# Attention and feed-forward layer: projections, bilinear keys and turns put into the 64-row and 64-column matmul shapes

## The chip, the cores and the metric

The kernel runs on 1 core of one Trainium2 chip. The metric is the device time of one execution in microseconds (us).

## The reference

Input x is 8 batches of 1024 rows of 256 numbers, all fp32. What is computed:

```python
x = x + attn(layernorm(x))          # 16 heads of 64, no mask
x = x + ffn(layernorm(x))

# attn: xn = layernorm(x) * gamma
q, k, v = xn @ Wq, split(xn @ Wkv)              # 256 -> 1024 each
q, k = rotary(q) / 8, rotary(k)
kt = einsum('bhnd,hde->bhne', k, W_bilinear)    # 64 x 64 per head
out = softmax(q @ kt.T) @ v                     # 1024 x 1024 per head
return out @ Wo
# ffn: layernorm, ternary w1 (256 -> 1024), gelu, layernorm, ternary w2
```

## The kernel before, in words

There are three stages. `prologue` normalises and turns the first batch and splits the projection weights into a high and a low part (each product of such operands is three fp32r matmuls: high by high, low by high, high by low). `feed_forward` runs over row tiles at the end. Between them stands `attention`, which the change is about.

`attention` runs over T = 64 pairs of heads (8 batches x 8 pairs). The loop body is `span(k, t, b)`, written out for each engine, and a span does three things at once, for different pairs: `attn` is the softmax and the value products of pair t, `prep` finds the row maxima of pair t + 1, and `proj` makes q, k, v of pair t + 2. In the first two spans (k = -2 and -1) there is no `attn`, in the last two no `proj`, so 62 spans do all three. A span has four quads (q = 0 to 3). On TensorE (the PE) each quad is, in this order:

- the score stage: 36 matmuls of 64 rows by 128 columns, issued in pairs for the two heads (L715 to L731 scores, L773 max scores). The eight max-score matmuls go to the banks X[0], X[1], M, X[0], X[1], M, X[0], X[1]; VectorE (DVE) reduces each (L654) and that frees the bank, which `x_red` counts.
- the projection stage, in 128 rows by 128 columns: K in q = 0 and Q in q = 1 (L834, 6 matmuls of 512 columns into M for the first half of the tokens, c = 0, then 6 into X[0] for the second, c = 1), V in q = 2 (L853, 12 matmuls of 256 columns into M, then 12 into X[0]) and two turns of the next x tile (L860), the bilinear keys in q = 3 (L877, one fp32 matmul into M, one into X[0]). q = 1 and q = 3 end with a turn of the maxima (L778).
- the value stage, in 128 rows by 64 columns, fp32: in q = 0 and q = 2 first the sums of the probabilities into M (L786), then 8 value products in pairs for the two heads (L910). An fp32 matmul shows as two records.

What releases what around the projections: DVE's `rotate` (L642 product with the cosines, L644 with the sines) reads c = 0 from M, then c = 1 from X[0]. The sums of q = 0 write M, and wait for `rotate` to have read it; the sums of q = 2 wait for ScalarE's copy of the c = 0 half of V (L514):

```python
if q == 0 and k >= 1:
    if proj:
        wait(pe, sin_made[K], 2 * pp + 1)
...
if q == 2:
    if proj:
        wait(pe, v_copied, 2 * pp + 1)
```

DVE then takes the reciprocal of the sums (L567). SyncE (SP) issues every DMA of the stage in one written order. GpSimd (POOL) adds the probabilities (L422), adds the rotated halves (L428) and multiplies the outputs by the reciprocals (L433).

## Time and profile before

| | |
|---|---|
| time, median of 3 runs | 3566.96 us (3565.94 to 3568.25) |
| span of the profiled execution | 3566.5 us |
| PE busy | 3472.3 us, 97% of the span |
| DVE busy | 2841.1 us, 80% |
| POOL busy | 2784.1 us, 78% |
| ACT busy | 2283.5 us, 64% |
| DMA | 321.71 MB, mean 90 GB/s |

The span is the time from the first to the last instruction of one profiled execution; no time of that execution beyond its span is given, and the median of the timed runs is 0.5 us above the span. Matmuls are pipelined: a record of PE lasts longer than the step from one matmul to the next, so the pace is read from the starts, and idle time of the PE is counted from the modelled end of the record before.

### The profile page before, as it was taken

How to read it: one execution, taken by the hardware profiler on the slowest of the kernel's cores; microseconds unless marked ns; L12 is line 12 of the kernel's file. 1: busy time of each engine (PE TensorE's matmuls, PEld its weight loads, DVE VectorE, ACT ScalarE, POOL GpSimd, SP SyncE). 2: the span in 40 equal slices, each digit the busy share in tenths (PEclk: the TensorE clock that was granted, in tenths of full speed). 3: DMA queues.
4: the chain of work that ended last, by engine and by line, in shares of the span. 5: the costliest groups of instructions: out<-in, count | busy, mean ns of one | idle time of the engine just before them, and what ended most of it. 6: DMA issues, size and time to landing. Idle time of an engine off the chain costs nothing. (4 is left out here: it accounts for less than half of the span.)

```text
span 3566.5 us, 70837 instructions
## 1 busy us (share of the span) xinstructions
PE 3472.3 (97%) x21150; PEld 2250.9 (63%) x21150; DVE 2841.1 (80%) x4376; ACT 2283.5 (64%) x4340; POOL 2784.1 (78%) x1407
## 2 busy tenths in 40 slices
PE   6999999999999999999999999999999996999999
PEld 4656655665555556555565555566666663888888
DVE  6778777778777777777777777887777777899998
ACT  2666666666666666666666666666666664555555
POOL 2999999999998899999999998999999995222222
PEclk8999999999999999999999999999999998999999
DMA  5222222222222222322222222222222112333332
GB/s 197 84 82 104 88 82 79 78 103 87 87 85 102 85 87 83 106 87 85 82 105 87 87 84 101 87 87 87 104 77 75 59 62 88 92 97 96 97 95 69
DMA packets 219697, 321.71 MB, mean 90 GB/s; under 512 B 20832, under 2 KB 144224, under 8 KB 214880
## 3 DMA queue, kind: packets, MB, share of 16 engines
q1 hardware_dynamic: 210144, 309.28, 25.5%
q10 hardware_dynamic: 9216, 8.39, 0.7%
q8 instruction: 156, 2.56, 0.3%
q14 instruction: 181, 1.48, 0.1%
HBM read 186.52 MB, written 61.60 MB: 70 GB/s over the span
## 5 line engine op out<-in xcount | busy, mean ns | idle before, releaser
L422 POOL TENSOR_TENSOR prob_sum<-prob_sum,prob 128x1024 f32<-128x1024 f32 x762 | 1883.6, 2472 | 248.0 <-ACT prob L506 204.7
L506 ACT ACTIVATE prob<-scores 128x512 f32<-128x512 f32 x2048 | 1072.0, 600 | 572.6 <-PE scores L724 557.8
L654 DVE TENSOR_REDUCE row_max<-max_scores 128x1 f32<-128x512 f32 x1536 | 988.3, 685 | 285.7 <-PE max_scores L773 267.7
L910 PE MATMUL attn_out<-prob,v 128*64 128x512 f32 x4096 | 930.8, 596 | 0.0
L715 PE MATMUL scores<-q_hi,k_hi 64*128 64x512 f32 x2048 | 782.6, 415 | 7.0 <-ACT scores L477 3.9
L724 PE MATMUL scores<-q_lo,k_hi 64*128 64x512 f32 x2048 | 752.8, 393 | 1.3 <-issue 1.3
L720 PE MATMUL scores<-q_hi,k_lo 64*128 64x512 f32 x2048 | 753.5, 394 | 0.0
L910 PEld LDWEIGHTS attn_out<-prob,v 128*64 128x64 f32 x4096 | 285.0, 137 | 557.5 <-issue 556.6
L773 PE MATMUL max_scores<-k_hi,q_hi 64*128 64x512 f32 x1536 | 578.1, 429 | 7.2 <-DVE rows L644 3.0
L477 ACT ACTIVATE scores<-neg_max_seeds 128x512 f32<-128x512 f32 x1024 | 553.3, 603 | 7.6 <-DMA neg_max_seeds<-neg_max_halves 7.6
L715 PEld LDWEIGHTS scores<-q_hi,k_hi 64*128 64x128 f32 x2048 | 376.4, 185 | 275.3 <-issue 159.0
L567 DVE RECIPROCAL sum_inverted<-shared 128x512 f32<-128x512 f32 x128 | 428.8, 3350 | 32.4 <-PE shared L786 32.3
L731 PE MATMUL scores<-neg_max,ones_rows 64*128 64x512 f32 x1024 | 397.1, 389 | 0.0
L724 PEld LDWEIGHTS scores<-q_lo,k_hi 64*128 64x128 f32 x2048 | 374.4, 185 | 24.8 <-issue 1.8
L720 PEld LDWEIGHTS scores<-q_hi,k_lo 64*128 64x128 f32 x2048 | 358.2, 185 | 16.0
L1044 POOL TENSOR_TENSOR up_scale<-veps_b,halfpow 128x1 f32<-128x1 f32 x64 | 35.1, 549 | 426.5 <-DVE up_biased L1173 402.7
L654 DVE TENSOR_REDUCE row_max<-shared 128x1 f32<-128x512 f32 x512 | 348.6, 681 | 0.1
L428 POOL TENSOR_TENSOR rows<-rows 128x1024 f32<-128x1024 f32 x128 | 305.3, 2385 | 28.3 <-DMA rows<-rows 28.3
L422 POOL TENSOR_TENSOR prob_sum<-prob 128x1024 f32<-128x1024 f32 x127 | 304.5, 2398 | 24.0 <-ACT prob L506 24.0
L773 PEld LDWEIGHTS max_scores<-k_hi,q_hi 64*128 64x128 f32 x1536 | 264.8, 185 | 42.3 <-DVE row_max L654 8.9
L834 PE MATMUL shared<-xt_batch,w_group 128*128 128x512 f32 x768 | 218.0, 420 | 11.8 <-issue 8.1
L773 PE MATMUL shared<-k_hi,q_hi 64*128 64x512 f32 x512 | 201.3, 393 | 0.3
(137 smaller groups left out, 5005.7 us busy)
## 6 DMA issues: line engine op xcount, KB each, us to landing
rows<-rows SPq DMA_DIRECT2D x512, 128.0 KB, 2.0
neg_max_seeds<-neg_max_halves SPq DMA_DIRECT2D x128, 512.0 KB, 3.8
w_group<-w_parts SPq DMA_DIRECT2D x30, 1536.0 KB, 6.9
attn_normalised<-z_stage SPq DMA_DIRECT2D x128, 256.0 KB, 2.0
v<-attn_normalised SPq DMA_DIRECT2D x64, 512.0 KB, 4.1
x_turned_parts<-x_tile_parts SPq DMA_DIRECT2D x49, 256.0 KB, 3.0
xt_batch<-x_turned_parts SPq DMA_DIRECT2D x7, 1792.0 KB, 11.2
x_in<-in_x SPq DMA_DIRECT2D x64, 128.0 KB, 3.8
```

The lines of the kernel that those rows point to most:

```text
L422: nc.gpsimd.tensor_tensor(psums[half][:, :, :], a, prob[:, n % RING, :, :], ALU.add).then_inc(added, 1)
L428: nc.gpsimd.tensor_tensor(rot[x][:, :], rot[x][:, :], swapped[x][:, :], ALU.add).then_inc(rot_made[x], 1)
L477: nc.scalar.activation(S[e][i][:, :], seeds[:, h, e, :], ACT.Copy).then_inc(seeded[e], 1)
L506: nc.scalar.activation(prob[:, n % RING, e, :], S[e][n % 2][:, :], ACT.Exp).then_inc(exped[e], 1)
L567: nc.vector.reciprocal(inv[:, :], M[:, :]).then_inc(inv_made, 1)
L654: nc.vector.reduce_max(mx[1 - u][:, e, n // 2, n % 2:n % 2 + 1], bank_of(e, jj)[:, :], axis=AX.X)\
L715: nc.tensor.matmul(out, KH[u][rows(e), keys], QH[u][rows(e), q], start=n % 4 >= SEEDED, stop=False, skip_group_check=True)
L720: nc.tensor.matmul(out, KL[u][rows(e), keys], QH[u][rows(e), q], start=False, stop=False, skip_group_check=True)
L724: last = nc.tensor.matmul(out, KH[u][rows(e), keys], QL[u][rows(e), q], start=False, stop=n % 4 < SEEDED, skip_group_check=True)
L731: nc.tensor.matmul(out, onesr[rows(e), :], NM[rows(e), q], start=False, stop=True, skip_group_check=True).then_inc(s_made[e], 1)
L773: nc.tensor.matmul(bank_of(e, jj)[:, :], QH[v][rows(e), tile * P:(tile + 1) * P], KH[v][rows(e), cols(part)], start=True, stop=True).then_ ...
L910: nc.tensor.matmul(O[rows(e), :], V[k // 2 % 2][:, j, col:col + DH], prob[:, n % RING, e, :], start=j == 0, stop=j == 7).then_inc(pv_made[ ...
```

## The change

Every matmul of the attention stage and of the prologue gets one of the two shapes of the score stage (64 rows by 128 columns) and the value stage (128 rows by 64 columns).

- The projections are cut into 64-row halves. Rows 0 to 63 of the array take the tokens of c = 0 and write M, rows 64 to 127 take those of c = 1 and write X[0]. The contraction over 256 is four steps of 64 (NK = 4) instead of two of 128, so K and Q are 12 pairs of matmuls each, and V is 24 pairs; the two halves are interleaved, c = 1 first. The wait ahead of them is one for both banks.
- Input (`XT`) and weights (`W`) are laid out for this: the input's upper partitions hold the second half of the tokens; the weights stand twice, in both halves of the partitions, so there is one buffer of 3 MB in place of two of 1.5 MB. It is refilled in three parts (`next_w`), each as soon as the projection that reads it is done.
- Keys, the turns of the maxima and of x are fp32 matmuls of 64 columns with the identity or the bilinear blocks, in place of full-width ones and of transposes.
- In the prologue only the first group of weights is split at once; three groups, in place of two, are split at the start of `attention` and written to memory in six DMAs each.

```diff
         @blk.tensor
         def _(pe):
-            pe.wait_ge(small_in, 32)
-            for u in two:
-                pe.wait_ge(x_normed, ST * (u + 1))
-                for k in range(KT):
-                    for i in range(ST):
-                        last = nc.tensor.transpose(bank[u][k][:, i * P:(i + 1) * P], xn[u][:, i, k * P:(k + 1) * P], ident[:, :])
-                last.then_inc(x_turned, 1)
+            pe.wait_ge(small_in, 48)
+            pe.wait_ge(x_normed, 2 * ST)
+            for k in quads:
+                for i in range(ST):
+                    for u in two:
+                        last = nc.tensor.matmul(bank[k][u * DH:(u + 1) * DH, i * P:(i + 1) * P],
+                                                xn[u][:, i, k * DH:(k + 1) * DH], ident[:, :], start=True, stop=True)
+                        if i == ST - 1:
+                            last.then_inc(x_turned, 1)
...
-            def load_w(group, u):
-                sp.dma_start(W[u][:, :, :, :].bitcast(F), w_scr[group]).then_inc(w_in[u], 16)
+            def load_w(group, x):
+                for c in two:
+                    sp.dma_start(W[rows(c), x].bitcast(F), w_scr[group, x]).then_inc(w_in[x], 16)
...
-                sp.dma_start(xt_scr[(b + (k + 2) // PAIRS - k // PAIRS + 1) & (B - 1), :, :, :, cols],
-                             xparts[k % 2][:, :, :, :].bitcast(F)).then_inc(x_stored[k % 2], 16)
+                for j in two:
+                    sp.dma_start(xt_scr[(b + (k + 2) // PAIRS - k // PAIRS + 1) & (B - 1), r // 4, :, :, j::2, cols],
+                                 xparts[k % 2][rows(j), :, :, :].bitcast(F)).then_inc(x_stored[k % 2], 16)
...
-                sp.dma_start(XT[:, :, :, 0:N - P].bitcast(F), xt_scr[b, :, :, :, 0:N - P]).then_inc(xt_in, 16)
+                for c, done in zip(two, (HALF, HALF - P)):
+                    sp.dma_start(XT[rows(c), :, :, 0:done].bitcast(F), xt_scr[b, c, :, :, :, 0:done]).then_inc(xt_in, 16)
...
+            def next_w(k, t, x):
+
+                p = (k + 2) % PAIRS
+                if p % 2 == 0 or k >= T - 3:
+                    return
+                for c in two:
+                    wait(sp, proj_made[x][c] if x < 2 else v_made[c], t + 3)
+                    at_rest()
+                group = (p // 2 + 1) % GROUPS
+                if k < PAIRS - 2:
+                    sp.wait_ge(w_out[group], 16 if group == 0 else 16 * 6)
+                load_w(group, 1 - x if x < 2 else 2)
+
+            def store_late(g):
+
+                wait_late(g)
+                for x in range(3):
+                    for j in two:
+                        sp.dma_start(w_scr[1 + g, x, :, :, j::2, :], stage[g % 2][rows(j), :, :, x * 2 * P:(x + 1) * 2 * P].bitcast(F))\
+                            .then_inc(w_out[1 + g], 16)
...
-                    if p % 2 and k < T - 6:
-                        wait(sp, v_made, 2 * (t + 2) + 2)
-                        at_rest()
-                        if k == -1:
-                            sp.wait_ge(w_out, 16 * GROUPS)
-                        load_w((p // 2 + 2) % (PAIRS // 2), (p // 2) % 2)
+                    next_w(k, t, 2)
...
-                    for g in two:
-                        sp.wait_ge(late_lo, g + 1)
-                        sp.dma_start(w_scr[2 + g], stage[g].bitcast(F)).then_inc(w_out, 16)
+                    store_late(0)
+                    sp.dma_start(late[0], late_src).then_inc(late_in[0], 16)
+                    store_late(1)
                     sp.wait_ge(zeroed, 5)
+                if k == -1:
+                    store_late(2)
             pairs(sp, span)
...
+                if k == -1:
+                    act.wait_ge(w_out[1], 16 * 6)
+                    late_high(2)
                 if k == 0:
-                    act.wait_ge(w_out, 16 * GROUPS)
+                    for g in (2, 3):
+                        act.wait_ge(w_out[g], 16 * 6)
...
-                            wait(act, v_made, 2 * (t + 2) + c + 1)
+                            wait(act, v_made[c], t + 3)
...
-                            tile = 4 * u + 2 * c
+                            tile = 4 * c + 2 * u
...
-                    wait(dve, proj_made[x], 2 * (t + 2) + c + 1)
+                    wait(dve, proj_made[x][c], t + 3)
...
-                nc.tensor.transpose(X[1][:, 0:P], negm[:, :], ident[:, :]).then_inc(nm_turned, 1)
+                nc.tensor.matmul(X[1][rows(0), 0:P], negm[:, rows(0)], ident[:, :], start=True, stop=True).then_inc(nm_turned, 1)
...
-                order = [(xp, wp, c) for xp, wp in ((0, 0), (1, 0), (0, 1)) for c in range(KT)]
+                order = [(xp, wp, c) for xp, wp in ((0, 0), (1, 0), (0, 1)) for c in range(NK)]
...
-                        for c in two:
-                            out = (M if c == 0 else X[0])[:, :]
-                            if q == K and c == 0:
-                                batch = b + (k + 2) // PAIRS - k // PAIRS
-                                if p % 2 == 0 and k > 0:
-                                    pe.wait_ge(w_in[p // 2 % 2], 16 * (2 * batch + p // 4))
-                                if p == 0 and k > 0:
-                                    pe.wait_ge(xt_in, 16 * batch)
-                                    wait(pe, x_stored[1], 64 * batch)
-                                wait(pe, lo_made[K], 2 * (t + 1) + 1)
-                                wait(pe, x_red[1], 16 * (t + 1) + 2)
-                            elif q == Q and c == 0:
-                                if not prep:
-                                    wait(pe, sin_made[K], 2 * pp + 1)
-                                wait(pe, x_red[1], 16 * (t + 1) + 6)
-                            else:
-                                wait(pe, x_red[1], 16 * (t + 1) + 4 * q + 3)
-                                if q == Q and not prep:
-                                    wait(pe, sin_made[K], 2 * pp + 2)
-                            base = 2 * P * (1 - q) + P * (p % 2)
-                            for m, (xp, wp, kt) in enumerate(order):
-                                last = nc.tensor.matmul(out, w[:, wp, kt, base:base + P], XT[:, xp, kt, cols(c)],
-                                                        start=m == 0, stop=m == len(order) - 1)
-                            last.then_inc(proj_made[q], 1)
+                        if q == K:
+                            batch = b + (k + 2) // PAIRS - k // PAIRS
...
+                            wait(pe, lo_made[K], 2 * (t + 1) + 1)
+                        if p % 2 == 0 and k > -2:
+                            pe.wait_ge(w_in[1 - q], 32 * (GROUPS * (b + (k + 2) // PAIRS - k // PAIRS) + p // 2))
+                        if q == Q and not prep:
+                            wait(pe, sin_made[K], 2 * pp + 2)
+                        wait(pe, x_red[1], 16 * (t + 1) + 4 * q + 3)
+                        for m, (xp, wp, kt) in enumerate(order):
+                            for c in (1, 0):
+                                last = nc.tensor.matmul((X[0] if c else M)[:, :], W[rows(c), 1 - q, wp, kt, P * (p % 2):P * (p % 2) + P],
+                                                        XT[rows(c), xp, kt, :], start=m == 0, stop=m == last_step)
+                                if m == last_step:
+                                    last.then_inc(proj_made[q][c], 1)
...
-                        for c in two:
-                            bank = M if c == 0 else X[0]
-                            if c == 0:
-                                if not prep:
-                                    wait(pe, sin_made[Q], 2 * pp + 1)
-                                wait(pe, x_red[1], 16 * (t + 1) + 10)
-                            else:
-                                wait(pe, x_red[1], 16 * (t + 1) + 4 * q + 3)
-                                if not prep:
-                                    wait(pe, sin_made[Q], 2 * pp + 2)
-                            for a in two:
-                                j = 4 * u + 2 * c + a
-                                for m, (xp, wp, kt) in enumerate(order):
-                                    last = nc.tensor.matmul(bank[:, a * 2 * P:(a + 1) * 2 * P], XT[:, xp, kt, j * P:(j + 1) * P],
-                                                            w[:, wp, kt, 4 * P:6 * P], start=m == 0, stop=m == len(order) - 1)
-                            last.then_inc(v_made, 1)
+                        if p % 2 == 0 and k > -2:
+                            pe.wait_ge(w_in[2], 32 * (GROUPS * (b + (k + 2) // PAIRS - k // PAIRS) + p // 2))
+                        if not prep:
+                            wait(pe, sin_made[Q], 2 * pp + 2)
+                        wait(pe, x_red[1], 16 * (t + 1) + 11)
+                        for a in two:
+                            j = (2 * u + a) * P
+                            for m, (xp, wp, kt) in enumerate(order):
+                                for c in (1, 0):
+                                    last = nc.tensor.matmul((X[0] if c else M)[:, a * 2 * P:(a + 1) * 2 * P], XT[rows(c), xp, kt, j:j + P],
+                                                            W[rows(c), 2, wp, kt, :], start=m == 0, stop=m == last_step)
+                                    if a and m == last_step:
+                                        last.then_inc(v_made[c], 1)
...
-                                last = nc.tensor.transpose(X[1][:, kt * P:(kt + 1) * P], xn[:, kt * P:(kt + 1) * P], ident[:, :])
+                                for j in two:
+                                    d = kt * P + j * DH
+                                    last = nc.tensor.matmul(X[1][rows(j), kt * P:(kt + 1) * P], xn[:, d:d + DH], ident[:, :],
+                                                            start=True, stop=True)
                             last.then_inc(x_turned, 1)
...
-                                nc.tensor.matmul((M if c == 0 else X[0])[:, :], WB[:, p, :], rot[K][:, cols(c)],
-                                                 start=True, stop=True).then_inc(kt_made, 1)
+                                for e in two:
+                                    nc.tensor.matmul((M if c == 0 else X[0])[rows(e), :], WB[:, p, rows(e)], rot[K][:, cols(c)],
+                                                     start=True, stop=True).then_inc(kt_made, 1)
...
-    w_scr = scr("w_parts", [GROUPS, P, 2, KT, GW])
-    xt_scr = scr("x_turned_parts", [B, P, 2, KT, N])
+    w_scr = scr("w_parts", [GROUPS, 3, DH, 2, NK, 2 * P])
+    xt_scr = scr("x_turned_parts", [B, 2, DH, 2, NK, HALF])
...
-        XT = sb("xt_batch", [P, 2, KT, N], R)
-        W = [sb(f"w_group{u}", [P, 2, KT, GW], R) for u in range(2)]
+        XT = sb("xt_batch", [P, 2, NK, HALF], R)
+        W = sb("w_group", [P, 3, 2, NK, 2 * P], R)
...
+            late_src = a["wqkv"].rearrange("(t p) g c -> g p t c", p=P)[3]
...
+        "gamma4": np.ascontiguousarray(np.tile(cols4(g["attn_gamma"]), (2, 1))),
```

## Rows read from the trace of the kernel before

**Rows 1.** The page: busy time of TensorE and the others.

```profile
PE 3472.3 (97%) x21150; PEld 2250.9 (63%) x21150; DVE 2841.1 (80%) x4376; ACT 2283.5 (64%) x4340; POOL 2784.1 (78%) x1407
```

**Rows 2.** Windows: the middle of the attention, and four quads of one span, summed.

```profile
86.00:2900.00 2814.00, 2803.86 (x16700) 1691.63 (x16698) 2216.35 (x3213) 1898.90 (x3665) 2561.77 (x1158) 1.00 0.25 87
```
```profile
sum 45.67, PE 45.59 PEld 27.29 DVE 36.28 ACT 31.05 POOL 41.83; mean PE 11.40 PEld 6.82 DVE 9.07 ACT 7.76 POOL 10.46
```

**Rows 3.** Timeline of PE, quad 0: start, time from first start to end, count.

```profile
1513.79 0.39 PE L731 MATMUL scores<-neg_max,ones_rows 64*128 64x512 f32 x1
1514.11 1.66 PE L834 MATMUL shared<-xt_batch,w_group 128*128 128x512 f32 x6
1515.60 1.54 PE L834 MATMUL max_scores<-xt_batch,w_group 128*128 128x512 f32 x6
1517.22 1.08 PE L786 MATMUL shared<-prob_sum,ones 128*64 128x512 f32 x4
```

**Rows 4.** Timeline of DVE in the same quad.

```profile
1513.98 0.69 DVE L654 TENSOR_REDUCE row_max<-max_scores 128x1 f32<-128x512 f32 x1 [0.21 <-PE max_scores L773]
1515.80 0.69 DVE L642 TENSOR_TENSOR rows<-shared,rows 128x512 f32<-128x512 f32 x1 [0.53 <-PE shared L834]
...
1516.41 0.68 DVE L644 TENSOR_TENSOR rows<-shared,rows 128x512 f32<-128x512 f32 x1
...
1518.39 3.35 DVE L567 RECIPROCAL sum_inverted<-shared 128x512 f32<-128x512 f32 x1
```

**Rows 5.** Timeline, all engines, where a score stage begins.

```profile
1521.66 0.49 PE L715 MATMUL scores<-q_hi,k_hi 64*128 64x512 f32 x1
...
1521.77 0.19 PEld L720 LDWEIGHTS scores<-q_hi,k_lo 64*128 64x128 f32 x1
1521.77 0.19 PEld L773 LDWEIGHTS max_scores<-k_hi,q_hi 64*128 64x128 f32 x1
1522.00 0.39 PE L720 MATMUL scores<-q_hi,k_lo 64*128 64x512 f32 x1
```

**Rows 6.** Timeline of PE and ACT, quad 2.

```profile
1537.39 1.70 PE L853 MATMUL shared<-w_group,xt_batch 128*128 128x256 f32 x12
1538.93 1.60 PE L853 MATMUL max_scores<-w_group,xt_batch 128*128 128x256 f32 x12
1540.37 0.38 PE L860 MATMUL max_scores<-ident,x_tile_normed 128*128 128x128 f32 x2
1540.68 1.08 PE L786 MATMUL shared<-prob_sum,ones 128*64 128x512 f32 x4
```
```profile
1539.13 0.60 ACT L514 ACTIVATE v<-shared 128x512 f32<-128x512 f32 x1 [0.97 <-PE shared L853]
```

**Rows 7.** Timeline of PE, quad 3.

```profile
1503.94 1.13 PE L877 MATMUL shared<-rows,wb_blocks 128*128 128x512 f32 x2
1504.90 1.02 PE L877 MATMUL max_scores<-rows,wb_blocks 128*128 128x512 f32 x2
1505.76 0.27 PE L778 MATMUL max_scores<-ident,neg_max_cols 128*128 128x128 f32 x1
1505.97 3.65 PE L910 MATMUL attn_out<-prob,v 128*64 128x512 f32 x16
```

**Rows 8.** Timeline of PE, last spans, which have no projections.

```profile
2973.48 0.39 PE L731 MATMUL scores<-neg_max,ones_rows 64*128 64x512 f32 x1
2973.80 1.51 PE L910 MATMUL attn_out<-prob,v 128*64 128x512 f32 x6
```

**Rows 9.** Timeline of PE, last spans: its idle times and what follows.

```profile
2956.74 0.33 PE L778 MATMUL max_scores<-ident,neg_max_cols 128*128 128x128 f32 x1 [1.31 <-DVE neg_max_cols L633]
```
```profile
2987.95 1.97 PE L786 MATMUL shared<-prob_sum,ones 128*64 128x512 f32 x4 [6.25 <-POOL prob_sum L422]
```

**Rows 10.** The start: PE's turns of x; DMAs, size and us to landing.

```profile
10.48 3.29 PE L151 MATMUL xt_bank<-ident,x_normed 128*128 128x128 f32 x16 [10.48 <-DVE x_normed L121]
```
```profile
w_parts<-prob SPq DMA_DIRECT2D x2, 1536.0 KB, 7.3
```

More of the change, by code:

```diff
@@ L26, with prologue @@
 ROUND = 1.5 * 2.0 ** 23
-def prologue(nc, x, wqkv, wbil, gamma, cos_in, ident_in, w_scr, XT, W, WB, late, late_in, tables, ident, gam, w_out):
-    STEPS, ST = 2, 4
-    two = range(2)
+def prologue(nc, x, wqkv, wbil, gamma, gamma4, cos_in, ident_in, w_scr, XT, W, WB, late, late_in, tables, ident, gam, w_out):
+    ST = 4
+    two, quads, parts = range(2), range(NK), range(3)
     with ExitStack() as ctx:
@@ L44, in prologue @@
         halfpow = sb("halfpow0", [P, ST], F)
-        bank = [[ctx.enter_context(nc.psum_tensor(f"xt_bank{u}{k}", [P, ST * P], F)) for k in range(KT)] for u in two]
-        x_in, w_in = [sem(f"x0_in{u}") for u in two], [sem(f"w0_in{g}") for g in two]
+        bank = [ctx.enter_context(nc.psum_tensor(f"xt_bank{k}", [P, HALF], F)) for k in quads]
+        x_in, w_in = [sem(f"x0_in{u}") for u in two], sem("w0_in")
         b_in, small_in, table_in, cleared = sem("b0_in"), sem("small0_in"), sem("tables0_in"), sem("wb0_cleared")
@@ L176, in adds_by, with attention @@
     return 7 * (n // 8) + max(n % 8, 1)
[L179 removed]
+def attention(nc, x, xt_scr, w_scr, z_scr, nm_scr, w_out, late, late_in, late_src, stage, XT, W, V, WB, prob, space, ident, gam, alpha, ffn_in, ffn_parts, next_loads):
     with ExitStack() as ctx:
@@ L234, in attention @@
         late_hi, late_lo = sem("w_late_hi"), sem("w_late_lo")
-        w_in, xt_in = [sem(f"w_in2{u}") for u in two], sem("xt_in2")
+        w_in, xt_in = [sem(f"w_in2{x}") for x in range(3)], sem("xt_in2")
         blk = ctx.enter_context(nc.Block())
@@ L457, in _, with late_high @@
                 act.sem_inc(s, CREDIT)
+            def late_high(g):
+                act.wait_ge(late_in[g % 2], 16 * (g // 2 + 1))
+                nc.scalar.activation(stage[g % 2][:, 0], late[g % 2], ACT.Copy).then_inc(late_hi, 1)
             for g in two:
-                act.wait_ge(late_in[g], 16)
-                nc.scalar.activation(stage[g][:, 0], late[g], ACT.Copy).then_inc(late_hi, 1)
+                late_high(g)
             def copy_z(t, h):
@@ L1264, in build @@
         alpha = sb("ffn_alpha", [P, 2], F)
-        w_out = ctx.enter_context(nc.semaphore("w_out"))
+        w_out = [ctx.enter_context(nc.semaphore(f"w_out{g}")) for g in range(GROUPS)]
         FW = DIM * HID // P
```

127 lines of the change are left out of this document (73 added, 54 removed).

## The prediction

> **What bounds the kernel now.** I read the page first. PE is busy 97% of the span, the others 80% or less [rows 1]; that is suspicious rather than final, since a PE record outlasts the step to the next. The windows settle it: in the middle 2814 us of the attention PE is busy 2803.86 us at the full clock (1.00, the 2.4 GHz level), and one whole span, taken as four quads, lasts 45.67 us with PE busy 45.59, POOL 41.83, DVE 36.28, ACT 31.05 [rows 2]. PE idles some 10 us in these 2814. So whatever lengthens or shortens PE's stream shows in full, 62 times over. POOL, next in line, has 3.8 us a span to spare, the others more.
>
> Then the timeline of one span, and in it the seams between the stages, because the change touches only what stands between score and value stage. Quad 0: the last pair of scores starts at 1513.79, the K projection at 1514.11, its second half at 1515.60, the sums at 1517.22 [rows 3]. Beside it DVE: the reduction of the seventh max score (bank X[0]) runs 1513.98 to 1514.67, that is, it ends 0.56 us after the projection has started; the cosines of c = 0 start at 1515.80 and the sines end at 1517.09, and the sums start 0.13 us after that [rows 4]. The two halves are staggered so that each hides a consumer: c = 0 in M runs while X[0] is still being reduced, and c = 1 runs while DVE reads M. This is where I look for the answer.
>
> **The multiplication itself: no change.** In a quad's scores the pairs step by 0.23 us (0.34 for the first of a stage, whose loads nothing hides [rows 5]), and six full-height 512-column matmuls take 1.54 us with a 0.39 us record, (1.54 - 0.39) / 5 = 0.23 [rows 3]. K and Q go from 12 matmuls to 12 pairs: 12 x 0.23 both ways, zero. V goes from 24 matmuls of 256 columns at (1.70 - 0.28) / 11, some 0.12 to 0.13 us each [rows 6] to 24 pairs. A 64-row pair of 256 columns is nowhere in the trace. Below: 0.12, if the two weight loads of a pair run side by side. Above: 0.23, the only step of a pair that is seen, which gives 24 x 0.11 = 2.6 us a span more. I take 0.12: where a score stage begins at 1521.66, both loads of the second pair start at 1521.77 [rows 5], so the two of the first pair were over within 0.11 us. The keys were 0.96 and 0.86 us [rows 7]; as pairs of 64 columns they are what the value products are, 3.65 us for 8, less the tail, or 0.86 a pair: zero.
>
> The Trainium skill (TensorE: Matmul & The Clock Gate, LDWEIGHTS) gives a load P / 1.2 ns for P columns, whatever the rows: 107 ns for 128, and the trace agrees with 0.11. If two such loads shared one port, that figure would make V 24 x 2 x 107 ns = 5.1 us in place of 2.9; that is the upper rival below under another name.
>
> **The seams of shape: a small gain.** Entering the 128-row shape from the scores costs 0.32 from start to start instead of 0.23 [rows 3]; entering the value shape straight from the scores costs the same, as the end of the attention shows: 2973.48 to 2973.80 [rows 8]. So one of three changes a quad goes away. Its price, from the turn to the value products: 0.20 [rows 7] against 0.11 for the turn alone, 0.09, and up to 0.05 of an unhidden load. The turns lose what they gain: as fp32 matmuls they are two passes of 128 columns, a quarter of 0.43 each, 0.21 for 0.11. Four seams a span make 62 x 4 x 0.09 = 22 us over the kernel at best. Quad 3, whose waits stay as they are, gains 0.1 us at most; elsewhere the sum is within 0.1.
>
> The Trainium skill (TensorEngine Tiling (Array Packing), Key Properties) says that a change of tiling mode drains TensorE, and gives no price. The trace shows the drain, and 0.09 us for it; by the rule alone the change would be a gain, of four drains a span, whatever one costs. It is the rule that speaks for a faster kernel.
>
> **The start wait, quads 0, 1 and 2: +0.62 us each.** The one wait ahead of the stage is `4 * q + 3`, for X[0], and c = 1 in X[0] goes first. What used to start at 1514.11 starts after 1514.67. From DVE's end to PE's start I have 0.13 for the sums, and zero as the lower bound; I take 0.06, so +0.62. Quads 1 and 2 have the same order of banks and reductions. All that is queued behind on PE moves with it.
>
> **The end wait, quad 0: +1.4 us.** Now both halves end together. From the first start to the last matmul is 1515.60 + 1.54 - 0.39 - 1514.11 = 2.64 us, as before. DVE takes up c = 0 0.43 us after its last matmul starts (1515.60 - 0.23 to 1515.80), then needs 0.61 + 0.68 = 1.29 us, and PE 0.13. The sums start at 1514.11 + 0.62 + 2.64 + 0.43 + 1.29 + 0.13 = 1519.22 instead of 1517.22: +2.00 in all. The wait of the sums on `sin_made[K]` isn't touched by the diff. In k = 0 there are no sums in quad 0. What is late next: `rotate` of c = 1 ends near 1520.4, the reciprocal (3.35 us, before at 1518.39) near 1523.7, and the next score stage starts near 1523.7 too and needs M only at its third max score, some 0.8 us on. No second stall.
>
> **The end wait, quad 2: +0.6 us.** The last V matmul starts at 1538.93 + 1.60 - 0.28 = 1540.25. ACT took up c = 0 0.32 us after its last one (1538.81 to 1539.13) and copies 0.60 us. Now: 1540.25 + 0.62 + 0.32 + 0.60 + 0.13 = 1541.92 for sums that started at 1540.68 [rows 6]: +1.24. The x turns, eight passes in four pairs now, 0.43 us, lie inside this wait; without it they would cost 0.2.
>
> **Quad 1: +0.65.** No sums follow; 0.62 and the longer turn.
>
> **DMAs.** The 31 loads of weights grow from 1.5 to 3 MB, some 46 MB more, in SP's queue at three places instead of one, two issues at each, in every second span. They are hidden: each part is free a span before it is needed. If that cover were gone, the first thing late would be the `max_rows` behind them in the queue, whose rows a score stage wants only two stages later.
>
> **Start.** Prologue turns: 32 of two passes in pairs, twice the 3.29 us of before [rows 10], and they wait for both input tiles to be normalised, another 1.4 us: +4.7. k = -2: nothing else hides the joint ends of K and Q: +3.5. k = -1: 3 x 0.6. The third late group is stored only at the end of k = -1 and ACT waits for it before its first exponential; such a store landed 7.3 us after issue [rows 10]: +8 with its six issues. Together +18, an estimate, 5 to 30.
>
> **Sum.** 2.00 + 0.65 + 1.24 - 0.10 = 3.79 a span; x 62 = 235, less 1.4 for k = 0: 234; with the start 252. The profiled span is 3566.5 and the median 0.5 above, so 3566.96 + 252 = 3818.
>
> **Rivals.**
> 1. As worked out, 3818. Its own bounds: latencies of 0 or 0.13 move the start waits by 3 x 0.07 x 62 = 13 each way, the start 13, an unhidden seam here or there 12: 3780 to 3860. Chance 0.72.
> 2. V pairs step at 0.23, by loads or by supply of instructions (four in 0.12 us; nothing in the trace is as dense): +2.6 x 62 = 164, 3980. For: not seen. Against: the loads of rows 5. Something between counts too: 3860 to 3980. Chance 0.12.
> 3. The new idle times, near 0.6, 1.9 and 1 us, lower PE's clock. After 6.25 us of idle the sums took 1.97 us where they take 1.08 [rows 3, 9], so the 1.2 GHz level; after 1.31 us the turn took 0.33 where it takes 0.27 [rows 7, 9], no halving. If 1.9 us did it in quad 0, the sums alone would cost 0.9 more, sums and half of the value products 2.7: 62 times that is 56 to 167, 3870 to 3980. Chance 0.07.
> 4. The start waits don't bind, because the reductions end sooner than in the span I read: 3 x 0.62 x 62 = 115 less, 3703. Against: the seventh reduction starts as its matmul ends, 0.2 us before the stage begins, and can't be earlier. With what lies between, 3650 to 3775: chance 0.06.
> 5. Faster. The drain would have to cost more than the seams show. One place, the removed change; 22 us by its row; the waits cost 234, so it decides only from 0.95 us a drain, ten times the row. Chance 0.02 for faster, 0.01 for no change (a measurement here tells 0.2%, 7 us, from none).
>
> The range holds rival 1 and the near halves of 2 and 3: 3775 to 3910. Slower 0.97.
>
> **What would show it.** Before the first projection matmul an idle of 0.5 us put down to DVE L654 in quads 0 to 2; before the sums of quad 0 one of 1.5 to 2 us put down to DVE's sines, before those of quad 2 one put down to ACT's copy of V; quad 3 unchanged or 0.1 shorter; a span of 49.5 us; PE's clock at 1.00. Wrong would be: V's pairs stepping above 0.12, a clock below 1.00 in the middle, or projections that start 0.23 us after the scores.

## The result, and the profile after

The changed kernel takes 3870.98 us (median of 4 runs, 3869.24 to 3873.36) where the kernel before takes 3566.45 (4 runs, 3565.37 to 3568.25): 304.5 us more, ratio 1.0854, 95% interval 1.0839 to 1.0870. Forecast were 3818 us, in a range of 3775 to 3910. So the time lies inside the range, and 53 us above the forecast. The profiled execution took 3873.36 us with a span of 3871.4.

The page's busy line:

```profile
PE 3530.1 (91%) x24990; PEld 2417.9 (62%) x24990; DVE 2840.5 (73%) x4377; ACT 2279.9 (59%) x4342; POOL 2787.3 (72%) x1408
```

DVE, ACT and POOL work as long as before, within 4 us [rows 1]. PE is busy 58 us more, but the span grew by 305: PE now stands still, and the question is where. First the windows: the middle of the attention, and below it the four quads of one span (in order 0 to 3), each from the first matmul of its scores to the first of the next, with their sum. The columns are the stretch, its length, the busy time of PE, PEld, DVE, ACT and POOL with the number of instructions, PE's granted clock as a share of full speed, the busy share of the DMA engines and the GB/s that they moved.

```profile
92.00:3150.00 3058.00, 2806.34 (x20002) 1816.13 (x20003) 2183.51 (x3172) 1866.81 (x3611) 2515.25 (x1138) 0.99 0.34 96
```
```profile
1726.66:1740.85 14.19, 12.12 (x81) 7.47 (x81) 10.74 (x13) 7.40 (x15) 10.30 (x5) 1.00 0.20 75
1740.85:1752.84 11.99, 11.36 (x80) 7.96 (x78) 9.49 (x16) 7.08 (x14) 9.52 (x5) 1.00 0.12 46
1752.84:1766.39 13.55, 12.74 (x114) 8.15 (x113) 8.50 (x11) 8.43 (x17) 13.47 (x7) 1.00 0.18 49
1766.39:1776.39 10.00, 10.00 (x64) 6.13 (x63) 7.53 (x15) 8.06 (x16) 8.57 (x5) 1.00 0.26 81
sum 49.73, PE 46.21 PEld 29.71 DVE 36.26 ACT 30.98 POOL 41.85; mean PE 11.55 PEld 7.43 DVE 9.07 ACT 7.75 POOL 10.46
```

The same four windows of the kernel before, whose sum alone stands in [rows 2]:

```profile
1509.55:1521.66 12.11, 12.03 (x70) 6.91 (x68) 10.73 (x13) 7.24 (x14) 10.97 (x5) 1.00 0.24 88
1521.66:1532.88 11.22, 11.22 (x68) 6.75 (x66) 9.51 (x16) 7.09 (x14) 8.75 (x5) 1.00 0.11 42
1532.88:1545.12 12.24, 12.24 (x84) 8.07 (x83) 8.38 (x11) 8.51 (x17) 12.16 (x6) 1.00 0.41 134
1545.12:1555.22 10.10, 10.10 (x60) 5.56 (x59) 7.66 (x15) 8.21 (x16) 9.94 (x6) 1.00 0.40 146
```

Quad 0 is 2.08 us longer, quad 1 0.77, quad 2 1.31, quad 3 0.10 shorter: 4.06 for this span (45.67 to 49.73). PE's busy time in it rose by 0.62 us (45.59 to 46.21), its idle time by 3.4, and the clock stayed at 1.00. The middle of the attention had some 10 us of idle PE; it has 3058.00 - 2806.34 = 252 now. The waits of PE over the attention (total us, times, longest) say what ended them:

```profile
PE shared L837 <- DVE rows L695: 88.0, 61, 1.5
PE max_scores L877 <- DVE row_max L705: 73.4, 124, 0.6
PE scores L766 <- ACT scores L524: 35.6, 9, 5.5
PE max_scores L893 <- DVE row_max L705: 34.9, 61, 0.6
PE shared L837 <- ACT v L565: 14.2, 55, 0.7
```

Four of the five are the forecast's start and end waits. The third, 9 waits of up to 5.5 us, is not in it. Then the timeline of PE in quad 0, which answers to [rows 3], and of DVE beside it [rows 4]:

```profile
1731.93 0.47 PE L877 MATMUL max_scores<-xt_batch,w_group 64*128 64x512 f32 x1 [0.62 <-DVE row_max L705]
1731.94 0.50 PE L877 MATMUL shared<-xt_batch,w_group 64*128 64x512 f32 x1
...
1734.57 0.39 PE L877 MATMUL shared<-xt_batch,w_group 64*128 64x512 f32 x1
1736.41 1.08 PE L837 MATMUL shared<-prob_sum,ones 128*64 128x512 f32 x4 [1.46 <-DVE rows L695]
```
```profile
1734.99 0.69 DVE L693 TENSOR_TENSOR rows<-shared,rows 128x512 f32<-128x512 f32 x1 [2.61 <-PE shared L877]
1735.60 0.68 DVE L695 TENSOR_TENSOR rows<-shared,rows 128x512 f32<-128x512 f32 x1
1737.56 3.36 DVE L618 RECIPROCAL sum_inverted<-shared 128x512 f32<-128x512 f32 x1
```

Both matmuls of the first pair start together, 0.62 us after PE ran dry; the last pair starts 2.63 us later (1734.57 - 1731.94). DVE takes up M 0.42 us after that, needs 1.29 us, and the sums start 0.13 us behind it. The chain is the one worked out in advance, link by link: 2.64, 0.43, 1.29, 0.13. The reciprocal ends at 1740.92, just after the next score stage has begun (1740.85), and no matmul of this stretch waits for it.

Quad 2 of the span before, PE: the second pair of V, the first matmul of the third pair, and the sums.

```profile
1708.51 0.28 PE L893 MATMUL max_scores<-w_group,xt_batch 64*128 64x256 f32 x1
1708.51 0.28 PE L893 MATMUL shared<-w_group,xt_batch 64*128 64x256 f32 x1
1708.63 0.28 PE L893 MATMUL max_scores<-w_group,xt_batch 64*128 64x256 f32 x1
...
1712.22 1.08 PE L837 MATMUL shared<-prob_sum,ones 128*64 128x512 f32 x4 [0.21 <-ACT v L565]
```

A pair of 64-row matmuls of 256 columns steps by 0.12 us (1708.51 to 1708.63), the lower of the two bounds. So the two weight loads of a pair don't add up to a longer step, and the second rival is out.

**Where a batch ends.** Seven of the nine waits for ACT's scores L524 stand at the ends of batches. One of them, SP's queue first (start, time to issue, count), then ACT and PE:

```profile
1604.74 1.13 SPq L287 DMA_DIRECT2D w_group<-w_parts  x2
1606.36 1.27 SPq L310 DMA_DIRECT2D xt_batch<-x_turned_parts  x2
...
1609.70 0.77 SPq L336 DMA_DIRECT2D neg_max_seeds<-neg_max_halves  x1
```
```profile
1624.45 2.15 ACT L524 ACTIVATE scores<-neg_max_seeds 128x512 f32<-128x512 f32 x4 [6.18 <-DMA neg_max_seeds<-neg_max_halves]
```
```profile
1625.11 0.79 PE L766 MATMUL scores<-q_hi,k_hi 64*128 64x512 f32 x1 [5.27 <-ACT scores L524]
...
1625.70 0.62 PE L771 MATMUL scores<-q_hi,k_lo 64*128 64x512 f32 x1
...
1626.12 0.62 PE L775 MATMUL scores<-q_lo,k_hi 64*128 64x512 f32 x1
```

The windows of that stretch, and under them the same place in the kernel before:

```profile
1608.00:1612.00 4.00, 4.00 (x28) 2.23 (x26) 3.79 (x4) 1.41 (x4) 2.87 (x2) 1.00 1.12 244
1612.00:1616.00 4.00, 4.00 (x29) 2.46 (x27) 3.43 (x7) 3.57 (x7) 3.93 (x3) 1.00 0.86 173
1616.00:1620.00 4.00, 3.83 (x20) 2.00 (x17) 2.05 (x5) 1.81 (x3) 3.92 (x2) 1.00 1.12 210
1620.00:1624.00 4.00, 0.00 (x0) 0.00 (x0) 0.00 (x0) 0.00 (x0) 2.82 (x2) 0.95 0.80 226
1624.00:1628.00 4.00, 2.90 (x14) 2.74 (x16) 1.90 (x3) 3.44 (x7) 0.00 (x0) 0.50 0.44 135
```
```profile
1080.00:1084.00 4.00, 4.00 (x32) 2.83 (x30) 3.92 (x6) 2.03 (x5) 4.00 (x2) 1.00 0.98 402
1084.00:1088.00 4.00, 4.00 (x23) 2.13 (x21) 3.27 (x6) 3.15 (x8) 3.92 (x4) 1.00 1.05 374
```

The seeds of half 0, a DMA of 512 KB that the very next score stage needs, are issued behind a third of the weights (1 MB), the next batch's input (1.75 MB) and a tile. ACT can use them 14.8 us after their issue. Before, 1.5 MB of weights and 1.75 MB of input stood ahead of them, more bytes, and it took 12.1 us (1079.29 to 1091.43). Most seeds are there 3.8 us after their issue (the median of all 128, in both kernels). In the four windows up to 1624 the DMA engines are 0.80 to 1.12 busy now and 0.98 to 1.05 before, but move 173 to 244 GB/s now and 374 to 402 before. What differs is the form: two transfers of 64 partitions for one of 128, and with it the length of the runs in them.

The Trainium skill (SBUF — State Buffer, Door 1: The DMA port swizzle) says that DMA bandwidth goes with the number of SBUF ports that the partitions of a transfer reach, and that 64 partitions on one side reach half of the ports. The trace agrees in direction, 173 to 244 against 374 to 402 GB/s; alone it doesn't separate this from the length of the runs.

After 5.27 us in which PE did nothing the clock is at 0.50, the 1.2 GHz level: the first pairs of scores step by 0.42 us (1625.70 to 1626.12) where they step by 0.23 at full clock.

**Where the difference lies in time.** The first reciprocal of the attention and one near its end, after and, under them, before:

```profile
145.07 3.35 DVE L618 RECIPROCAL sum_inverted<-shared 128x512 f32<-128x512 f32 x1
...
3253.18 3.36 DVE L618 RECIPROCAL sum_inverted<-shared 128x512 f32<-128x512 f32 x1 [0.35 <-PE shared L837]
```
```profile
117.65 3.35 DVE L567 RECIPROCAL sum_inverted<-shared 128x512 f32<-128x512 f32 x1
...
2947.55 3.36 DVE L567 RECIPROCAL sum_inverted<-shared 128x512 f32<-128x512 f32 x1 [0.68 <-PE shared L786]
```

27.4 us are lost up to the first, 305.6 up to the last; what comes behind it takes 1 us less than before. So the spans between cost 278.2 us. The first reciprocal stands in quad 2 of k = 0, so 27.4 is the start and some 2.4 us of that first span.

### The profile page after: what moved, and what is told of

The parts are those of the page before. It is cut to its first block and busy times, and to the rows that moved or that the text cites. A ratio compares the mean times of both kernels' runs of the same rounds, so it can differ in the third digit from the quotient of the medians.

```text
span 3871.4 us, 79185 instructions
## 1 busy us (share of the span) xinstructions
PE 3530.1 (91%) x24990; PEld 2417.9 (62%) x24990; DVE 2840.5 (73%) x4377; ACT 2279.9 (59%) x4342; POOL 2787.3 (72%) x1408
## 2 busy tenths in 40 slices
DMA packets 236691, 373.37 MB, mean 96 GB/s; under 512 B 24736, under 2 KB 156320, under 8 KB 223648
## 5 line engine op out<-in xcount | busy, mean ns | idle before, releaser
L955 PE MATMUL attn_out<-prob,v 128*64 128x512 f32 x4096 | 953.8, 595 | 0.0
L766 PE MATMUL scores<-q_hi,k_hi 64*128 64x512 f32 x2048 | 790.7, 419 | 43.6 <-ACT scores L524 35.6
L955 PEld LDWEIGHTS attn_out<-prob,v 128*64 128x64 f32 x4096 | 408.4, 137 | 411.5 <-issue 293.5
L524 ACT ACTIVATE scores<-neg_max_seeds 128x512 f32<-128x512 f32 x1024 | 553.9, 605 | 39.0 <-DMA neg_max_seeds<-neg_max_halves 39.0
L877 PE MATMUL max_scores<-xt_batch,w_group 64*128 64x512 f32 x1536 | 390.2, 401 | 86.8 <-DVE row_max L705 74.3
L877 PE MATMUL shared<-xt_batch,w_group 64*128 64x512 f32 x1536 | 394.4, 403 | 0.0
L877 PEld LDWEIGHTS max_scores<-xt_batch,w_group 64*128 64x128 f32 x1536 | 278.9, 188 | 160.4 <-issue 104.0
```

The costliest lines, as they stand in the source:

```text
L524: nc.scalar.activation(S[e][i][:, :], seeds[:, h, e, :], ACT.Copy).then_inc(seeded[e], 1)
L766: nc.tensor.matmul(out, KH[u][rows(e), keys], QH[u][rows(e), q], start=n % 4 >= SEEDED, stop=False, skip_group_check=True)
L877: last = nc.tensor.matmul((X[0] if c else M)[:, :], W[rows(c), 1 - q, wp, kt, P * (p % 2):P * (p % 2) + P], XT[rows(c), xp, kt, :], start= ...
L955: nc.tensor.matmul(O[rows(e), :], V[k // 2 % 2][:, j, col:col + DH], prob[:, n % RING, e, :], start=j == 0, stop=j == 7).then_inc(pv_made[ ...
```

## The experiments

All times are medians. A difference is against the kernel before as it ran on the same chip (3565.6, 3567.0 and 3567.2 us for the three sets). The changed kernel stands at +304.5 on that scale. The bounds behind a ratio are its 95% interval. In the kernels made from the changed one, all else stays.

### The start wait alone (b_start)

The kernel before, in its old shapes, with the wait of the first half put where the wait of the second is:

```diff
-                                wait(pe, x_red[1], 16 * (t + 1) + 2)
+                                wait(pe, x_red[1], 16 * (t + 1) + 3)
...
-                                wait(pe, x_red[1], 16 * (t + 1) + 6)
+                                wait(pe, x_red[1], 16 * (t + 1) + 7)
...
-                                wait(pe, x_red[1], 16 * (t + 1) + 10)
+                                wait(pe, x_red[1], 16 * (t + 1) + 11)
```

> The kernel before, with one thing changed: the projections of quads 0, 1 and 2 wait for the reduction of the bank X[0] before their first half too, as the changed kernel does. Theory (the waits set the cost): three start waits of 0.6 us in 62 spans, 112 us more, 3678 us; the projection's first matmul starts 0.6 us later after the scores. Rival (the wait is hidden, or the new shapes cost the time): no change, 3566 us.

Measured: 3681.75 us, +116.2, ratio 1.0326 (1.0308 to 1.0343), or 1.87 us a span if all of it is put there: three times 0.62. A span costs a little less, since the first reciprocal is already 5.2 us late (122.81 against 117.65). Its waits:

```profile
PE shared L834 <- DVE row_max L654: 69.8, 122, 0.7
PE shared L853 <- DVE row_max L654: 31.4, 61, 0.6
```

They answer to the changed kernel's 73.4 and 34.9. No shape has changed here, so the one wait on both banks is enough for 116 of the 304 us. The fourth rival, that this wait doesn't bind, is refuted.

### Start and end waits, in the old shapes (b_joined)

The kernel before with its halves interleaved, as the changed kernel does it, but in 128 rows by 128 columns and with the old layouts and DMAs (K and Q shown, V likewise):

```diff
+                        wait(pe, x_red[1], 16 * (t + 1) + 4 * q + 3)
+                        for m, (xp, wp, kt) in enumerate(order):
+                            for c in two:
+                                last = nc.tensor.matmul((X[0] if c else M)[:, :], w[:, wp, kt, base:base + P], XT[:, xp, kt, cols(c)],
                                                         start=m == 0, stop=m == len(order) - 1)
+                                if m == len(order) - 1:
+                                    last.then_inc(proj_made[q], 1)
```

> The kernel before, shapes, layout and DMAs as they were, but the projections joined as in the changed kernel: one wait for both banks, and the two halves interleaved matmul by matmul, so that they end together. Theory: the whole loss of a span comes from this order, 4.0 us (the 3.94 us of the changed kernel's span and the 0.1 us that its shapes save), times 62: 248 us more, 3814 us, with the idle before quad 0's sums near 1.5 us. Rival (64-row halves, their drains or their DMAs cost it): 3566 us, or only the 112 us of the start waits, 3678 us, if the joint end is hidden.

Measured: 3788.77 us, +223.2, ratio 1.0624 (1.0606 to 1.0642). Besides the waits of the run above it has the end waits:

```profile
PE shared L786 <- DVE rows L644: 72.9, 60, 1.2
...
PE shared L786 <- ACT v L514: 26.6, 61, 0.6
```

The joint end adds 107.0 us. Start and end wait together are +223.2 with no matmul in a new shape, so the order in which the halves are made costs some three quarters of the slowdown. Between its first reciprocal (130.78, or 13.1 late) and the one near the end (3169.11, or 221.6 late) this run loses 208 us, 3.4 a span. The run falls 25 us short of the 3814 that its expectation gave: interleaved, M's last matmul is one step earlier than in the pairs, and the sums wait 1.2 us here, 1.46 there. That is 16 us over 62 spans. It also leaves something for the new shapes: the changed kernel loses 3.9 us a span (worked out below), 0.5 more than this run, of which the longer wait is 0.26 and a slower turn in quad 1 some 0.1. No run takes the rest apart.

### Keys and second turn of the maxima alone (b_keys)

The one part of the change that leaves every wait as it is, put into the kernel before:

```diff
-                                nc.tensor.matmul((M if c == 0 else X[0])[:, :], WB[:, p, :], rot[K][:, cols(c)],
-                                                 start=True, stop=True).then_inc(kt_made, 1)
+                                for e in two:
+                                    nc.tensor.matmul((M if c == 0 else X[0])[rows(e), :], WB[:, p, rows(e)], rot[K][:, cols(c)],
+                                                     start=True, stop=True).then_inc(kt_made, 1)
...
+                if h:
+                    nc.tensor.matmul(X[1][rows(0), 0:P], negm[:, rows(0)], ident[:, :], start=True, stop=True).then_inc(nm_turned, 1)
+                    return
```

> The kernel before, with the one part of the change that meets no new wait: keys and the turn of the maxima of quad 3 as 64-column matmuls; everything else as before. Theory: the shape change between turn and value products goes, quad 3 takes 10.01 us instead of 10.10, 0.09 us in 62 spans, 5.6 us less: 3560 us. Rival: pairs of 64 columns cost what the drain saves: 3565.6 us.

Measured: 3561.05 us (11 runs, against 18 of the kernel before), -6.0, ratio 0.9986 (0.9977 to 0.9995). This is the seam of quad 3: 62 x 0.1 = 6.2 us. The 64-column shape does gain where the next stage already has it and nothing is waited for. In quads 0 and 2 PE waits at the seam anyway, so a removed drain should only turn into idle time there; that is argued, no run isolates it.

### The seeds ahead of the large loads (a_seeds)

SP issues the seeds of half 0 before the third of the weights and the input, not behind them:

```diff
                         load_x(t + 1, k + 1, b + (k + 1) // PAIRS - k // PAIRS)
+                    if prep:
+                        max_seeds(t, 0)
                     next_w(k, t, 2)
...
                 if prep:
-                    max_seeds(t, 0)
+                    if not proj:
+                        max_seeds(t, 0)
```

> The changed kernel, with SyncE issuing the seeds of the first half (max_seeds(t, 0)) ahead of the loads of V's weights and of the next batch's input instead of behind them. Theory: the seven spans at the end of a batch lose 5 to 8 us because those seeds land behind the input's loads, and 2 to 3 us of that is PE's clock after the idle; out of the queue's way they cost nothing: 38 to 45 us less, about 3829 us. Rival: the DMA engines are full then whatever the order, so another transfer is late in place of this one and the seven spans keep half or all of their loss: 3850 to 3871 us.

Measured: 3827.58 us, +262.0, ratio 1.0733 (1.0715 to 1.0751): 42.5 us come back, 6.1 for each of seven batches. Of PE's 35.6 us for ACT's scores this is left:

```profile
PE scores L769 <- ACT scores L527: 2.6, 2, 2.4
```

So the loads are as large as before and land even later (the first half of the input 13.5 us after its issue, 10.5 in the changed kernel, by the page), and yet PE no longer waits behind them. The seeds are 512 KB themselves; what counts is that they are wanted first, and what was wrong was who stands behind whom in the queue.

### The same move in the kernel before (b_keys_seeds)

b_keys and the edit above together. It asks how much of those 42.5 us the kernel before already paid.

> The same, and also the seeds of the first half issued ahead of the loads at the end of a batch. In the kernel before those seven spans are 0.9 to 1.9 us longer than the others, with ACT waiting 7.2 us in all for the seeds. Theory: both gains add, 5.6 and 7 us: 3553 us, faster than both kernels. Rival for the second part: the loads take the engines either way and something else is late: 3560 us.

Measured: 3556.22 us (8 runs), -10.8, ratio 0.9972 (0.9961 to 0.9982). The move is worth 4.8 us there, so the change added some 42.5 - 4.8 = 38 us at the ends of the batches. This version is the fastest of all that ran.

### The input load in 128 partitions (a_xt_whole)

```diff
-                for c, done in zip(two, (HALF, HALF - P)):
-                    sp.dma_start(XT[rows(c), :, :, 0:done].bitcast(F), xt_scr[b, c, :, :, :, 0:done]).then_inc(xt_in, 16)
+                sp.dma_start(XT[:, :, :, 0:HALF - P].bitcast(F),
+                             xt_scr[b].rearrange("c d s k n -> (c d) s k n")[:, :, :, 0:HALF - P]).then_inc(xt_in, 16)
+                sp.dma_start(XT[rows(0), :, :, HALF - P:HALF].bitcast(F), xt_scr[b, 0, :, :, :, HALF - P:HALF]).then_inc(xt_in, 16)
```

> The changed kernel, with the next batch's input loaded by one DMA over all 128 partitions (384 of the 512 columns of both halves) and one small one for the rest of the first half, in place of one DMA for each half of the partitions. Bytes are the same and the pieces are no longer (1.5 KB instead of 2 and 1.5 KB). Theory: transfers into 64 partitions are what makes the DMA engines move 210 GB/s here where they moved 400 GB/s in the kernel before; the big load lands 3 to 5 us sooner, the seeds behind it too, and the seven batch ends lose 25 to 40 us less: about 3840 us. Rival: the shorter pieces (2 and 1.5 KB in place of 3.5 KB) are what makes them slow: no change, 3871 us.

Measured: 3847.62 us, +280.6, ratio 1.0791 (1.0774 to 1.0807): 24 of the 38 us, with some 6 us of noise either way, by the form of one load that moves the same bytes from the same place in the queue. Two windows in which it runs, and what ACT still waits for the seeds (39.0 us, 7 times, longest 6.4 in the changed kernel):

```profile
1596.00:1600.00 4.00, 4.00 (x32) 2.75 (x30) 3.80 (x6) 2.04 (x5) 2.82 (x2) 1.00 0.99 256
1600.00:1604.00 4.00, 4.00 (x28) 2.26 (x26) 3.26 (x6) 3.11 (x8) 4.00 (x3) 1.00 1.12 316
```
```profile
ACT scores L525 <- DMA neg_max_seeds<-neg_max_halves: 17.4, 7, 3.3
```

At the same busy share of 1.12 the engines move 316 GB/s instead of 210 to 244. The pieces of this load are shorter than those of the halves (runs of 384 elements, where the first half was read in one unbroken run of 4096 a partition), and the page counts more packets, 243411 against 236691, or 960 more for each of the seven loads. So short runs don't explain the slow halves; the partitions are left as the likelier cause. The Trainium skill (DMA: Bandwidth & Descriptors, Rules for kernel authors) says that two transfers to disjoint halves of the partitions run one after the other, and advises one of 128 in their place; this run agrees, with 24 us. The weights still came in halves here, so the full 402 GB/s isn't to be expected.

### The sums later in the value stage (a_sums)

The wait for `rotate` and for V's copy stands ahead of the sums, and the value products queue behind it though they need neither. Here two of quad 0's four steps of value products go first, and one of quad 2's:

```diff
                         for jj in range(4):
+                            if q == 0 and jj == 2 and k >= 1:
+                                if proj:
+                                    wait(pe, sin_made[K], 2 * pp + 1)
...
+                                sums(t - 1, 1)
+                            if q == 2 and jj == 1:
+                                if proj:
+                                    wait(pe, v_copied, 2 * pp + 1)
...
+                                sums(t, 0)
```

> The changed kernel, with the sums moved into the value stage: in quad 0 after two of the four steps of value products, in quad 2 after one, so that PE has work while DVE reads M and ACT copies V. Theory: PE's idle there (1.46 and 0.21 us) goes, but DVE's reciprocal (3.35 us) can't start earlier and its eight reductions come behind it, so that the next score stage and the projection after it win only 0.4 to 0.6 us a span: 25 to 37 us less, about 3840 us. Rival (only PE counts, DVE has room): 1.67 us a span, 104 us less, 3767 us.

Measured: 3834.17 us, +268.6, ratio 1.0757 (1.0739 to 1.0775): 36 us back, a third of the 102 that these two waits hold. The place of the wait has moved:

```profile
PE shared L824 <- DVE sum_inverted L618: 57.2, 61, 1.1
```
```profile
1717.37 3.36 DVE L618 RECIPROCAL sum_inverted<-shared 128x512 f32<-128x512 f32 x1 [0.28 <-PE shared L837]
```
```profile
1720.88 0.47 PE L824 MATMUL shared<-k_hi,q_hi 64*128 64x512 f32 x1 [0.97 <-DVE sum_inverted L618]
```

The sums wait for nobody now, but their reciprocal holds M until 1720.73, and the third max score of the next stage needs M: 0.97 us of idle. The chain through M (projection, rotate, sums, reciprocal, max score) is nearly as long as the quad, so moving the sums back on PE doesn't hide the joint end.

### The third store earlier (a_store)

```diff
+                    if k == -1:
+                        store_late(2)
                     next_w(k, t, 2)
...
-                if k == -1:
-                    store_late(2)
```

> The changed kernel, with the third late group of weights stored in the span k = -1 before V's weights are fetched instead of at that span's end, where ACT waits 8.3 us for it before its first exponential. Theory: those 8 us go and PE's clock doesn't fall behind them, 8 to 12 us less, 3861 us. Rival: the wait is replaced by another at the start (seeds, queue): 3868 to 3871 us.

Measured: 3864.01 us, +297.0, ratio 1.0834 (1.0818 to 1.0851): 7.5 us back, and ACT's single wait of 8.3 us for the store is gone. The forecast's term for it was 8.

### All three repairs (a_all)

The edits of a_seeds, a_sums and a_store in one kernel.

> The changed kernel with three edits that were each measured alone: the seeds ahead of the loads (43 us less), the sums inside the value stage (37 us less), the third late group stored sooner (7 us less). Theory: they act at different places and add, 87 us less: 3784 us, still 6% slower than the kernel before, because the start waits (3 x 0.6 us a span) and most of the end wait stay. Rival: the seeds and the sums pay for the same idle, 3795 us or more.

Measured: 3779.88 us, +212.7, ratio 1.0592 (1.0574 to 1.0610). 92 us come back where the three alone give 42.5 + 35.9 + 7.5 = 86: within the noise of these runs they add. What stays is mostly the start waits (71.5 and 34.3 us of PE's waits) and the new wait for the reciprocal (58.2).

## Why the prediction was right, and where it was short

The direction, the place and the mechanism of the spans were right. The number was 53 us low: 38 at the ends of the batches, 7 at the start, some 7 in the spans. The first rival by itself, with its own bounds, went to 3860 only, and 3871 lies above them. The full range held the time because it also took in the near halves of the second and third rival, V's pairs at a longer step and a lower clock in the spans, and neither came true; that it was in range is in part luck.

**The failed step: "They are hidden: each part is free a span before it is needed."** That looked at the weights, which are indeed in time. It did not look at what stands behind them in SP's queue for the same score stage. The forecast named `max_rows`, wanted two stages later; the seeds of half 0 stand behind them too and are wanted at once. It also took the new loads for as fast as the old, because it counted bytes and never asked how many partitions a transfer reaches. Seven times 5.4 us, not 62 times something, is a pattern that no window over one ordinary span shows: the span that was read had no input load in it. a_seeds shows that the place behind the loads costs the time, and a_xt_whole that the form of the input load alone makes 24 of the 38 us.

**The terms of a span.** Forecast were +2.00, +0.65, +1.24, -0.10; the span above shows +2.08, +0.77, +1.31, -0.10, or 49.73 us where 49.5 were forecast. Over all spans, 278.2 us less 38 for the batch ends is 240, or 3.9 a span, against 3.79. The multiplication at zero: confirmed, V's pairs step by 0.12. The start wait: 0.62 forecast, 0.62 in the row, at most 1.87 for three in b_start. The end wait: 88.0 / 61 = 1.44 us in quad 0, and in quad 2 14.2 us over 55 times, 0.26, with the longer x turns filling the rest, as forecast. No second stall behind the reciprocal: right, by a margin so narrow that sums moved later make one (a_sums). Quad 1 was undersized by 0.12: its turn is now entered from the 64-row shape, 0.32 us after the last projection matmul (1748.73 to 1749.05), where it followed its own shape after 0.23 before. No run isolates that; it is read from rows alone. The seam at 0.09: confirmed by b_keys (6.0 us over 62 spans).

**The start: 18 forecast, 25 measured.** From the starts of PE's stages, after less before: first K projection 25.65 against 21.85 us, +3.8 (forecast 4.7); second K projection 57.34 against 47.98, so k = -2 cost 5.6 (forecast 3.5); keys of k = -1 93.94 against 78.57, so three quads cost 6.0 (forecast 1.8); third K projection 116.17 against 90.50, 10.3 (forecast 8). Of these 10.3 us, 7.7 are PE's wait for ACT's exponentials, which wait for the late store, and 0.6 is the start wait of k = 0; the other 2.0 are longer busy time, at a granted clock of 0.61 for 0.73.

The most undersized term is k = -1, at 0.6 a quad. These spans have no value products, and so nothing lies between the joint end of a projection and the next score stage: its first max score waits for `rotate`, 2.58 and 2.24 us in quads 1 and 2, where it waited 1.38 and 1.61 before.

```profile
64.30 0.79 PE L824 MATMUL max_scores<-k_hi,q_hi 64*128 64x512 f32 x1 [2.58 <-DVE rows L695]
```

In the ordinary spans the value stage hides just that. But the idle time is the smaller part. The same three quads, after and, under them, before:

```profile
57.34:93.94 36.60, 28.59 (x131) 18.42 (x131) 22.71 (x37) 3.95 (x7) 8.68 (x4) 0.64 0.71 194
```
```profile
47.98:78.57 30.59, 23.77 (x76) 14.76 (x76) 22.68 (x38) 2.58 (x6) 4.72 (x2) 0.83 0.32 114
```

PE is idle 1.2 us longer and busy 4.8 us longer, and its granted clock is 0.64 where it was 0.83: it spent more of the stretch at the 1.2 GHz level, and that is most of the longer busy time. The forecast priced the waits of k = -1 and not the clock. That the longer waits brought the clock down is argued from their order in time; no run isolates it.

**The sum again, from the runs:** 25 at the start, 62 x 3.9 - 1.4 = 240 in the spans, 38 at the batch ends: 303 of 304.5. The 3.9 comes from the changed kernel's own times, so this shows where the time lies and is no second measurement.

**The rivals.** V's pairs at 0.23: no. A lower clock: not in the spans, with their waits of 0.6 and 1.5 us (1.00 in all four quads), but after the unforeseen 5.27 us at the batch ends it was at 0.50; those 5 us at half speed are part of the 38. In k = -1 it was lower than before, and up to 4.8 us go with that. Start waits that don't bind: refuted by b_start. Faster by drains: the saving is real and 6 us large, in the one quad where nothing is waited for.

**What stays open.** Whether the slow loads are slow for their partitions alone; a_xt_whole speaks for it but changes only one of two loads. No time was measured for a shorter reduction of the seventh max score (32 of its 512 columns), which should shorten the start wait. Why k = -2 cost 2.1 us more than forecast was not taken apart either.

## What to carry to other kernels

Two halves that are made one after the other can hide each other's consumers; packing them side by side cost nothing in the multiplication here and gave up that overlap, so before changing a shape, list what runs between the two halves and what each bank's next user waits for. When bulk transfers grow or change form, look at what stands behind them in the queue and at how soon each of it is wanted, in the rarest kind of iteration too, and issue what is wanted soonest first. Read the start of the kernel apart from its steady state: with little to fill the waits there, PE's clock fell too, and in k = -1 its longer busy time cost more than its idle time. A saved drain was worth 0.1 us at a seam where the engine didn't wait for anything else.

## What the runs showed of the hardware that was not expected

- In windows in which the DMA engines were 0.80 to 1.12 busy, loads in halves of 64 partitions moved 173 to 244 GB/s (210 and 244 in the two at 1.12); loads in 128 partitions moved 374 and 402 at 1.05 and 0.98, a mixture 256 and 316 at 0.99 and 1.12.
- After 5.27 us of idle PE ran at 0.50 of the clock, with pairs of scores at 0.42 us for 0.23; with idle times up to 1.46 us in a span it was at 1.00 in all four quads, and it is 0.99 on average from 92 to 3150 us. In k = -1, with idle times of 2.58 and 2.24 us among others, it was 0.64 on average.
- Two 64-row matmuls of 256 columns with a weight load each, on the two halves of the array, step by 0.12 us a pair: one full-height matmul of 256 columns steps no faster.
